# Three of every 128 gathered groups of rows loaded by single-row DMAs from ScalarE and SyncE

## The reference: one layer of attention over a graph

```
Q, K, V = x @ Wq + bq, x @ Wk + bk, x @ Wv + bv        # per node, as 8 heads of 12
Ee      = edge_attr @ We + be                          # per edge
score   = K[src] * Q[dst] / sqrt(12) * Ee
score   = exp(clip(score.sum(-1), -5, 5))              # per edge and head
wV      = segment_sum(V[src] * score, dst)
Z       = segment_sum(score, dst)
out     = layernorm(x + wV / (Z + 1e-6))
```

## Time and profile before

| | |
|---|---|
| median of 3 runs | 4183.3 us (4180.95 to 4184.16) |
| the profiled execution | 4178.04 us, span 4176.2 us |
| busy share of the span | GpSimd 75%, TensorE 73%, its weight loads 71%, VectorE 65%, ScalarE 34% |
| DMA engines, mean busy share | 0.75 to 0.76 in the middle of the loop |
| mean granted TensorE clock | 0.509 of full speed |

### The profile page before, as it was taken

How to read it: one execution, slowest core, us unless ns; L and a number is a source line. 1 busy time by engine, 2 the same in 40 slices (tenths; PEclk the granted TensorE clock), 3 DMA queues, 4 the chain that set the end, 5 groups by cost and what they waited for, 6 DMA issues and landing times.

```text
span 4176.2 us, 61383 instructions
## 1 busy us (share of the span) xinstructions
PE 3048.5 (73%) x16776; PEld 2960.0 (71%) x16777; DVE 2698.4 (65%) x6866; ACT 1402.5 (34%) x3656; POOL 3134.1 (75%) x3361
## 2 busy tenths in 40 slices
PE   7797777777777777777777777777777777777775
PEld 7797677777677677777677677776777677776674
DVE  4786666666666666666666666666666666666666
ACT  3443333333333333333333333333333333333335
POOL 7777777777777777777777777777777777777775
PEclk8555555555555555555555555555555555555555
DMA  9897777777777777777777777777777777777763
GB/s 264 168 156 138 134 133 131 132 134 134 131 130 133 135 133 131 132 133 135 131 130 133 134 134 130 132 134 135 131 131 132 134 134 130 131 134 133 133 123 111
DMA packets 1533399, 570.88 MB, mean 137 GB/s; under 512 B 1392683, under 2 KB 1453788, under 8 KB 1533365
## 3 DMA queue, kind: packets, MB, share of 16 engines
q1 hardware_dynamic: 1369107, 237.47, 37.3%
q0 software_dynamic: 156832, 321.69, 37.3%
q10 hardware_dynamic: 7426, 11.35, 0.8%
HBM read 547.37 MB, written 22.87 MB: 137 GB/s over the span
## 4 chain that ended last, share of the span: by engine, by line
POOL 62%; issue 22%; DVE 5%; DMA 5%; PE 1%; POOLq 1%; DVEq 0%; ACT 0%; ACTq 0%
POOL kv_mem L608 62%; DMA kv_mem<-kv_table,src_idx 5%; DVE kqe L1056 1%; DVE msg_mem L1069 1%; DVE kqe L1053 1%; DVE eaT L1076 1%; PE bank L721 0%; DVE y_stats L1169 0%; POOLq L52 0%; PE bank L732 0%; DVE oh L1065 0%; POOLq L605 0%; DVE raw_score L1060 0%; DVE accT L1050 0%; DVE mean_var L1182 0%
## 5 line engine op out<-in xcount | busy, mean ns | idle before, releaser
L608 POOL DMA_INDIRECT kv_mem<-kv_table,src_idx x3224 | 3049.8, 946 | 991.3 <-issue 971.7
L721 PE MATMUL bank<-w_e,eaT 97*128 97x96 f32 x6448 | 1624.5, 434 | 1057.2 <-DVE eaT L1076 1055.6
L721 PEld LDWEIGHTS bank<-w_e,eaT 97*128 97x128 f32 x6448 | 1446.1, 329 | 1125.1 <-DVE eaT L1076 1114.0
L732 PE MATMUL bank<-oh,msg_mem 128*104 128x32 f32 x6448 | 1258.1, 359 | 6.2 <-DVE msg_mem L1069 6.2
L732 PEld LDWEIGHTS bank<-oh,msg_mem 128*104 128x104 f32 x6448 | 1211.2, 293 | 6.7 <-DVE msg_mem L1069 6.7
L1053 DVE TENSOR_TENSOR kqe<-kv_mem,bank 128x384 f32<-128x384 f32 x806 | 444.5, 551 | 1071.7 <-DMA kv_mem<-kv_table,src_idx 1067.3
L848 ACT ACTIVATE msg_mem<-score 128x32 f32<-128x32 f32 x806 | 184.7, 229 | 2651.8 <-DVE score L1083 2650.0
L854 ACT ACTIVATE away<-off_mem,minus_row 96x512 bf16<-96x512 uint8 x806 | 568.8, 706 | 2.0 <-issue 2.0
L1076 DVE STREAM_TRANSPOSE eaT<-ea_mem 96x512 f32<-96x512 f32 x806 | 564.4, 700 | 0.0
L857 ACT ACTIVATE ohT<-away 96x512 bf16<-96x512 bf16 x806 | 507.2, 629 | 25.4
L1056 DVE TENSOR_TENSOR kqe<-kqe,bank 128x384 f32<-128x384 f32 x806 | 446.2, 554 | 27.8
(11 more groups left out here) (96 smaller groups left out, 509.8 us busy)
## 6 DMA issues: line engine op xcount, KB each, us to landing
ea_mem<-in_edge_attr_dram SPq DMA_DIRECT2D x603, 256.0 KB, 7.8
kv_mem<-kv_table,src_idx POOLq DMA_INDIRECT x3224
off_mem<-offset_by_chunk SPq DMA_DIRECT2D x201, 204.0 KB
q_win<-q_table SPq DMA_DIRECT2D x806, 19.9 KB
kv_table<-kv_mem SPq DMA_DIRECT2D x25, 336.0 KB
q_table<-msg_mem ACTq DMA_DIRECT2D x25, 252.0 KB
x_res<-in_x_dram SPq DMA_DIRECT2D x25, 168.0 KB
out_dram<-kv_mem SPq DMA_DIRECT2D x25, 168.0 KB
```

The lines of the kernel that those rows point to most:

```text
L608: pool.indirect_dma_start(kv[:, slot, g, :], None, kv_dram[:, :], bass.IndirectOffsetOnAxis(ap=src_idx[:, u % IDX_RING, g:g + 1], axis=0)) ...
L721: nc.tensor.matmul(e_ps[v][:, g * D:(g + 1) * D], eaT[:, v, g * P:(g + 1) * P], w_e[:, :], start=True, stop=True)
L732: last = nc.tensor.matmul(sums_of(s, v), msg[:, w, g, :], oh[:, w % DEPTH, g, :], start=(g == 0), stop=(g == G - 1), skip_group_check=True)
```

## The change

Three of the 128 groups in each 32 chunks (`BLOCK`) are no longer gathered by GpSimd: the last group of the block's chunk 15 and the last two groups of its chunk 31. This holds for the 25 whole blocks (800 chunks). Their rows are loaded one by one, each by a DMA whose row number was read into a register. SyncE loads chunk 15's: the row numbers at one half round, then 19 rows at the end of each of the next seven half rounds. ScalarE loads chunk 31's 256 rows: the row numbers at the end of step 0 of the block, then nine rows at the end of each step from 1 on. The rows go into buffers of their own (`sp_rows`, `act_rows`); VectorE waits for them and makes the product and the messages of chunks 15 and 31 in two instructions each, one per buffer. The loops are unrolled over 32 steps instead of 16. A separate table of bases is replaced by a row of an existing one.

```diff
+BLOCK = 32
+SP_CHUNK = 15
+ACT_CHUNK = 31
+ACT_GROUPS = 2
+SP_STEP = 19
+ACT_STEP = 9
+ROW_LOAD = 10
...
+        gathered = {SP_CHUNK: G - 1, ACT_CHUNK: G - ACT_GROUPS}
...
+        def load_rows(engine, first, last, idx, rows, landed):
+
+            for p0 in range(first, last, ROW_LOAD):
+                count = min(ROW_LOAD, last - p0)
+                nodes = nc.values_load_multi_w_load_instructions(
+                    idx[0:1, p0:p0 + count], engines=(engine.engine,), min_val=0, max_val=N - 1,
+                    skip_runtime_bounds_check_because="sources are numbers of nodes")[1]
+                for r, node in zip(range(p0, p0 + count), nodes):
+                    engine.dma_start(rows[r % P:r % P + 1, r // P, :].rearrange("a (r d) -> a r d", r=4),
+                                     kv_dram[bass.ds(node, 1), :].rearrange("a (r d) -> a r d", r=4)).then_inc(landed[r % len(landed)], 16)
...
+            def take_rows(s, u):
+
+                phase = (u + BLOCK - SP_CHUNK - 1) % BLOCK
+                chunk = s - u + SP_CHUNK + (BLOCK if u > SP_CHUNK else 0)
...
+                if phase == 0:
+                    load_row_sources(sp, chunk, 1, sp_idx, sp_idx_in)
+                else:
+                    k = phase // HALF - 1
+                    if k == 0:
+                        sp.wait_ge(sp_idx_in, ((chunk - SP_CHUNK) // BLOCK if isinstance(s, int) else block_now[0] + 1) * 32 + 32)
+                        if not isinstance(chunk, int) or chunk > BLOCK:
+                            sp.wait_ge(msg_ready, chunk - BLOCK + 1)
+                        sp.sem_inc(sp_rows_allowed, 1)
+                    load_rows(sp, k * SP_STEP, min(P, (k + 1) * SP_STEP), sp_idx, sp_rows, sp_rows_in)
...
+            for u in range(SP_CHUNK + 1 + HALF - BLOCK, HALF, HALF):
+                take_rows(u, u)
...
-                for g in range(G):
+                for g in range(gathered.get(u, G)):
 
                     pool.indirect_dma_start(kv[:, slot, g, :], None, kv_dram[:, :],
...
                 if u % IDX_GROUP == 0 and (not isinstance(s, int) or s > 0):
                     copy_sources(s + IDX_AHEAD, (u + IDX_AHEAD) % IDX_RING)
...
+                if not isinstance(s, int) or 0 <= s < WHOLE:
+                    first = s - u
+                    if u == 0:
+                        load_row_sources(act, first + ACT_CHUNK, ACT_GROUPS, act_idx, act_idx_in)
+                    if u == 1:
+
+                        act.wait_ge(act_idx_in, (first + BLOCK) * (ACT_GROUPS * 32 // BLOCK))
+                        if not isinstance(first, int) or first > 0:
+                            act.wait_ge(msg_ready, first)
+                        act.sem_inc(act_rows_allowed, 1)
+                    lo, hi = (u - 1) * ACT_STEP, min(u * ACT_STEP, ACT_GROUPS * P)
+                    if u >= 1 and lo < hi:
+                        load_rows(act, lo, hi, act_idx, act_rows, act_rows_in)
...
+                    if here < G:
+                        for rows_in in sp_rows_in if u == SP_CHUNK else act_rows_in:
+                            dve.wait_ge(rows_in, block * (8 * P) + 8 * P)
+                        rows = sp_rows if u == SP_CHUNK else act_rows
+                        nc.vector.tensor_tensor(kqe[:, here:G, :], rows[:, :, 0:D],
+                                                q_ps[v][:, here * D:G * D].rearrange("p (g d) -> p g d", g=G - here), ALU.mult)
```

More of the change, by code:

```diff
@@ L161, in gnn_kernel @@
         lohi_end_i = sb("lohi_end_i", [1, 4], I32)
-        base_tab = sb("base_tab", [1, C], I32)
         base_all = sb("base_all", [P, C], I32)
+        base_tab = base_all[0:1, :]
         extra_tab = sb("extra_tab", [1, C], I32)
         most = sb("most", [1, 1], I32)
+        act_idx = sb("act_idx", [1, ACT_GROUPS * P], I32)
+        act_rows = sb("act_rows", [P, ACT_GROUPS, 2 * D])
+        sp_idx = sb("sp_idx", [1, P], I32)
+        sp_rows = sb("sp_rows", [P, 1, 2 * D])
         rel = sb("rel", [P, C * G], I16)
@@ L269, in gnn_kernel @@
         kv_in = [sem(f"kv_in{i}") for i in range(KV_RING)]
+        act_idx_in = sem("act_idx_in")
+        act_rows_allowed = sem("act_rows_allowed")
+        act_rows_in = [sem(f"act_rows_in{i}") for i in range(2 * ACT_GROUPS)]
+        sp_idx_in = sem("sp_idx_in")
+        sp_rows_allowed = sem("sp_rows_allowed")
+        sp_rows_in = [sem(f"sp_rows_in{i}") for i in range(2)]
         pe_step = sem("pe_step")
@@ L419, in load_offsets, with load_row_sources @@
                 "(a c r) -> a c r", a=1, c=count).to_broadcast((SEL_LOAD, count, CHUNK))).then_inc(off_b_in[h], 16)
+        WHOLE = C // BLOCK * BLOCK
+        gathered = {SP_CHUNK: G - 1, ACT_CHUNK: G - ACT_GROUPS}
+        def load_row_sources(engine, chunk, groups, idx, landed_sem):
+            edge = chunk * CHUNK + (G - groups) * P
+            for h in range(2 * groups):
+                engine.dma_start(idx[:, h * 64:h * 64 + 64].bitcast(I32),
+                                 src[bass.ds(edge + h * 64, 64)].rearrange("(a r) -> a r", a=1)).then_inc(landed_sem, 16)
+        def load_rows(engine, first, last, idx, rows, landed):
[7 more added lines that the diff above has]
+                                     kv_dram[bass.ds(node, 1), :].rearrange("a (r d) -> a r d", r=4)).then_inc(landed[r % len(landed)], 16)
         def load_x(engine, b, h):
@@ L478, in _ @@
             load_edges(sp, 2 * EA_GROUP, 2)
+            wait_all(sp, kv_stored)
+            load_row_sources(sp, SP_CHUNK, 1, sp_idx, sp_idx_in)
+            for u in range(SP_CHUNK + 1 + HALF - BLOCK, HALF, HALF):
+                take_rows(u, u)
             groups = RING // HALF
-            rounds = (C - AHEAD) // RING
+            rounds = (C - AHEAD) // BLOCK
             lead = AHEAD // HALF
-            for s in range(HALF, RING, HALF):
-                half_round(s, (s // HALF + lead) % groups, None)
+            for s in range(HALF, BLOCK, HALF):
+                half_round(s, (s // HALF + lead) % groups, None, s)
             with sp.Fori(1, rounds) as i:
-                for g in range(groups):
+                block_now[:] = [i]
+                for g in range(BLOCK // HALF):
                     if g % 2 == 0:
[L488 to L491, removed]
+                        bases = load_bases(sp, i * BLOCK + g * HALF + AHEAD)
+                    half_round(i * BLOCK + g * HALF, (g + lead) % groups, bases[g % 2 * HALF:g % 2 * HALF + HALF], g * HALF)
+            for s in range(rounds * BLOCK, C - AHEAD, HALF):
+                half_round(s, (s // HALF + lead) % groups, None, s % BLOCK)
             sp.wait_ge(most_ready, 1)
@@ L610, in step @@
                                             ).then_inc(kv_in[slot], 16)
-            run_steps(pool, step, C, 0, first=4)
+            run_steps(pool, step, C, 0, unroll=BLOCK, first=2)
             def gather(c):
@@ L862, in step @@
                     copy_sources(s + IDX_AHEAD, (u + IDX_AHEAD) % IDX_RING)
-            run_steps(act, step, C, 1, lead=DEPTH, ahead=IDX_RING + EA_GROUP)
+                if not isinstance(s, int) or 0 <= s < WHOLE:
[10 more added lines that the diff above has]
+                        load_rows(act, lo, hi, act_idx, act_rows, act_rows_in)
+            run_steps(act, step, C, 1, lead=DEPTH, unroll=BLOCK, ahead=IDX_RING + EA_GROUP)
             def further(c, extra):
@@ L1051, in step @@
                 if scores:
-                    landed(dve, kv_in, a, ua, 16 * G, u)
-                    nc.vector.tensor_tensor(kqe[:, :, :], kv[:, ua, :, 0:D],
-                                            q_ps[v][:, 0:G * D].rearrange("p (g d) -> p g d", g=G), ALU.mult).then_inc(kq_done, 1)
+                    here, block = gathered.get(u, G), a // BLOCK if isinstance(a, int) else block_now[0]
+                    if u in gathered:
+                        before = 0 if u == SP_CHUNK else 16 * gathered[SP_CHUNK]
+                        dve.wait_ge(kv_in[ua], block * (16 * sum(gathered.values())) + (before + 16 * here))
+                    else:
+                        landed(dve, kv_in, a, ua, 16 * G, u)
+                    if here < G:
[4 more added lines that the diff above has]
+                                                q_ps[v][:, here * D:G * D].rearrange("p (g d) -> p g d", g=G - here), ALU.mult)
+                    nc.vector.tensor_tensor(kqe[:, 0:here, :], kv[:, ua, 0:here, 0:D],
+                                            q_ps[v][:, 0:here * D].rearrange("p (g d) -> p g d", g=here), ALU.mult).then_inc(kq_done, 1)
                     dve.wait_ge(kq_done, a + 1)
@@ L1068, in step @@
                     weights = weight_ps[um % DEPTH].rearrange("p (g h) -> p g h", g=G)
-                    nc.vector.tensor_tensor(msg[:, um % MSG_RING, :, 0:D].rearrange("p g (h d) -> p g h d", d=HD),
-                                            kv[:, um, :, D:2 * D].rearrange("p g (h d) -> p g h d", d=HD),
```

(13 more changed lines are left out.)

18 lines of the change are left out of this document (12 added, 6 removed).

## The result

The changed kernel takes 5402.7 us (median; 5399.94 to 5406.09) against 4182.7 us: ratio 1.2917 [1.2895, 1.294], 29% slower. The forecast was 4687 us and the range ended at 5000. The profiled execution's span is 5404.2 us at a granted clock of 0.507.

What follows compares the result with a forecast made beforehand. GpSimd's gathers bound the kernel before, ScalarE after: 1.07 + 0.79 + 3.96 = 5.82 us a row step, 178 us a block; 25 blocks plus five steps give 4470 us against 3966.0, 504 more, so 4687 us; whole range 4085 to 5000.

Steps and rivals of the forecast that it cites:

- What bounds the kernel: GpSimd's gathers, 1.25 us apart, bound it before; ScalarE becomes the bound at 5.82 us a row step against 4.89.
- The register load: ScalarE's one load of nine source numbers in each row step costs 0.79 us, ends 0.55 and 2.1.
- The row: Each single-row DMA on ScalarE with its address arithmetic costs 0.44 us, ends 0.41 and 0.49; nine are 3.96 us.
- The step's own chain: ScalarE from its exponentials through line 857, with the step's register work and next wait, takes 1.07 us.
- The block's turn: Around it 3.6 steps go at VectorE's 3.37 us; code loading for the longer loops was left in the margin.
- SyncE: Its rows and register loads add 9.9 us a half round; a block takes 154 to 177 us, covered by ScalarE's 178.
- Rival 1: ScalarE's row loads fit and GpSimd stays the bound: 4089 us, needing a row at 0.36 us; 12%.
- Rival 2: SyncE is the bound, at 166 us a block, if ScalarE's rows and loads are cheap: 4388 us; 10%.
- Rival 3: ScalarE's register load goes at VectorE's price, 2.1 us instead of 0.79: a step of 7.13 us, 5603 us in all; 18%.

Runs made afterwards that it cites:

- experiment 8: Changed kernel with ScalarE's part alone, rows of fixed numbers, without register loads or address arithmetic (wrong rows loaded): 4128.3 us, ratio 0.9854.
- experiment 10: Changed kernel with one ScalarE group, four rows in steps 1 to 26, eight in 27 to 29, no SyncE rows: 4147.6 us against 4178.8, ratio 0.9929.
- Experiment 3: Changed kernel with ScalarE's part alone, each step's nine numbers 12 apart so every load begins on a multiple of four: 4658.4 us, ratio 1.1121.
- experiment 5: Kernel before plus register loads of 1 to 12 values from different places, each value used by a copy, ending ScalarE's and VectorE's programs: 4217.3 us, measured once.
- experiment 2: Changed kernel with SyncE's part alone, ScalarE's two groups back on GpSimd: 4654.6 us, ratio 1.1112.
- experiments 6: Changed kernel with one ScalarE group, eight rows in 16 steps, loads on multiples of four, no SyncE rows: 4170.1 us against 4189.5, ratio 0.9957.
- 7: Changed kernel with one group each on ScalarE (eight rows a step) and SyncE (20 a half round), loads on multiples of four: 4510.4 us, ratio 1.0777.

## Why the prediction was wrong

- **What bounds the kernel: right.** GpSimd before (experiments 8 and 10 give back what its gathers cost, 1.25 us each), ScalarE after, with the waits passed on from one-hot to messages to gathers as foreseen.
- **"The register load: … I take SyncE's price with its gaps, 0.79 us": this step failed.** It was 0.96 us in one step of four and 2.14 in three. Over 28 full steps that is 51.7 us, with gaps of 0.04 some 52.8, where the forecast has 28 x 0.79 = 22.1: 31 us more, and the block of 206.4 us exceeds the forecast's 178 by 28. The rows (-7.5) and the turn (+4.5), below, make up the difference. I saw both prices in the earlier trace rows and read them as two engines. SyncE's eight numbers begin on multiples of eight and VectorE's do not; the changed kernel's nine a step begin on a multiple of four only once in four. Experiment 3 takes this away and lands near the forecast's block, in part by luck, as said there; experiment 5 shows that the place decides on either engine.
- **The row: somewhat cheaper.** 37 + 29 + 228 ns and three gaps are 0.385 us, against 0.44 and a lower end of 0.41; the first after a load takes 0.235 more (its issue is 463 ns). A block: 256 x 0.385 + 28 x 0.235 = 105.1 us for 112.6. Of the lower end, 0.24 of issue and 0.17 of arithmetic and gaps, both parts were a little high (0.228 and 0.157); I took more because a load of a single row had shown 0.30.
- **The step's own chain: right.** 1.00 us to the load's start and 0.04 before the next exponentials, for 1.07.
- **The block's turn: not priced, and not nothing.** I left code loading in the margin, for no row showed it. The three steps around the turn take 1.98 + 6.23 + 6.37 = 14.6 us instead of 3 x 3.37 = 10.1: 4.5 us a block, 112 us in the run. Both ScalarE and VectorE pause at their branches, but the rows put the price on VectorE's pause: in all 22 turns ScalarE's exponentials after the two pauses start 0.03 us behind VectorE's score, and VectorE's one-hot ahead of that score did not wait for ScalarE. No run takes either pause away alone.
- **SyncE: right in kind, at the top of its range by luck.** 154 to 177 us was the range, 176.7 is the block where SyncE alone decides. The upper 22.7 us were put down to rows held up behind the edge loads; but the loads took 26.4 us a block instead of 14 x 0.76 = 10.6, for the same reason as ScalarE's, and the first row after a load only 0.19 us more than the others in the mean (0.416 against 0.228), 2.6 us a block. And the start was not hidden: VectorE waited 19.5 us for SyncE's first rows, at 265.8 us.
- **Rival 1** (the rows fit) fell for the change. A row at 0.385 misses its 0.36; experiment 8 shows that it would have come true without loads and arithmetic. **Rival 2** (SyncE) holds for the change's other half alone (4654.6 us; it said 4388), and is hidden behind ScalarE. **Rival 3** named the mechanism: a load near VectorE's price. It gave 5603 us with every load at 2.1; the quarter of short ones and the cheaper rows, against the dearer turn, make 5403. My reason against it, the single load that goes with SyncE's, said nothing on loads of nine.

## What to carry to other kernels

A register load of several values is priced by where its first value lies: start it on a multiple of four 32-bit numbers and round the count to fours, and it costs a half or less. Before taking over work from a busy engine, sum what the new engine's sequencer does for each piece, its arithmetic and its loads, and spread the pieces so thin that the longest step stays under that of the engine behind it: four rows a step, with the eight-row steps last, gave the whole 31 us of which eight gave 19. When two rows of a profile price the same operation differently, find what differs between the two operands before putting it down to the engine.

## What the runs showed of the hardware that was not expected

- The register load, as above: 8 values in 0.55 us from a multiple of four, 1.77 from elsewhere (ScalarE).
- A loop's branch can cost what four gathers do. ScalarE's loop has 94 recorded instructions in the kernel before (0.21 us from the branch to the next instruction), 179 in experiment 2 (0.20), 447 in experiment 8 (5.9 in the median), 585 in experiments 6 (4.9) and 7 (2.7) and 988 in the changed kernel (5.20); SyncE's has 212 in experiment 8 (0.26) and 618 in experiment 2 (2.6); VectorE's has 201 in the kernel before (0.20) and 405 to 409 in the changed kernel and experiments 2 and 7 (4.2, 3.0 and 4.5). Where GpSimd is the bound, as in experiments 8 and 10, the pauses cost no time. With the long loops the queue q14 moves code between 1000 and 3500 us (266 packets in the changed kernel), and before it moves none in the loop. The Trainium skill, "Runtime: NRT & Kernel Launch", section "Instruction fetch mechanics", says that a taken branch to code outside the two blocks that an engine holds (512 instructions for most) has to fetch it first. The rows agree in kind; that 405 are already too long may be due to waits, which the records leave out, and no run varies the length alone.
- The first small DMA after a register load takes 0.463 us to issue on ScalarE, the next ones 0.228 (0.448 and 0.213 in experiment 3). It comes with every load there, on whatever place; its cause was not tried.
